# An LSTM layer on one core: gates regrouped into four equal banks, the cell state by a scan, x injected once per chunk

## What is computed

```
xW = einsum('ntd,dk->tnk', x, Wx) + b
a = xw_t + prev_h @ Wh                      # (4, 1024)
i = sigmoid(a[:, 0:H]);      f = sigmoid(a[:, H:2*H])
o = sigmoid(a[:, 2*H:3*H]);  g = tanh(a[:, 3*H:4*H])
next_c = f * prev_c + i * g
next_h = o * tanh(next_c)
return x + transpose(hs, (1, 0, 2))
```

## Time and profile before

| | |
|---|---|
| device time, median of 3 runs | 1141.09 us (1139.99 to 1141.9) |
| span of the profiled execution | 1138.7 us |
| instructions | 90172 |
| TensorE matmuls / weight loads busy | 915.0 us / 689.1 us |
| VectorE / ScalarE busy | 774.7 us / 395.4 us |
| DMA traffic | 8.72 MB, mean 8 GB/s |

### The profile page before, as it was taken

One profiled execution on the slowest core, in us unless ns is written; L12 is line 12 of the kernel. 1 busy time (PEld: TensorE's weight loads), 2 busy tenths in 40 slices (PEclk: granted clock), 3 DMA queues, 4 the chain that ended last, 5 costly groups with the idle time before them and its releaser, 6 DMA issues.

```text
span 1138.7 us, 90172 instructions
## 1 busy us (share of the span) xinstructions
PE 915.0 (80%) x38912; PEld 689.1 (61%) x38912; DVE 774.7 (68%) x4896; ACT 395.4 (35%) x2562; POOL 0.7 (0%) x6
## 2 busy tenths in 40 slices
PE   1888888888888888888888888888888888888886
PEld 1666666666666666666666666666666666666664
DVE  2676676676766766766766666767667666667665
ACT  0333333333333333333333333333333333333332
POOL 0000000000000000000000000000000000000000
PEclk9999999999999999999999999999999999999999
DMA  2000000000000000000000000000000000000000
GB/s 82 6 6 6 5 5 7 5 5 7 5 6 6 5 6 6 5 6 6 5 6 5 5 7 5 5 7 5 6 6 5 6 6 5 6 6 5 6 5 6
DMA packets 31868, 8.72 MB, mean 8 GB/s; under 512 B 31344, under 2 KB 31344, under 8 KB 31856
## 3 DMA queue, kind: packets, MB, share of 16 engines
q1 hardware_dynamic: 31248, 8.41, 3.1%
q10 hardware_dynamic: 608, 0.14, 0.1%
HBM read 6.43 MB, written 2.10 MB: 7 GB/s over the span
## 4 chain that ended last, share of the span: by engine, by line
DVE 42%; PE 39%; ACT 8%; issue 7%; DMA 2%; SPq 0%; DVEq 0%
PE gates L373 28%; DVE cell_bank L285 14%; DVE prods L290 9%; DVE cell_bank L303 8%; ACT acts L198 7%; PE gates_o L361 7%; DVE acts L297 5%; PE x_acc L343 5%; DVE h_units L308 3%; DVE x_part L226 2%; DMA wh_raw<-in_L_cond_Wh_dram 2%; DVE h_rows L261 1%; ACT cell_bank L206 1%; SPq L142 0%; SPq L136 0%
## 5 line engine op out<-in xcount | busy, mean ns | idle before, releaser
L373 PE MATMUL gates<-wh,h_units 128*4 128x96 f32 x16384 | 433.2, 247 | 49.9 <-DVE h_units L308 46.1
L373 PEld LDWEIGHTS gates<-wh,h_units 128*4 128x4 f32 x16384 | 311.1, 86 | 153.5 <-DVE h_units L308 149.2
L285 DVE STREAM_TRANSPOSE cell_bank<-gates 128x96 f32<-128x96 f32 x1024 | 243.0, 277 | 231.5 <-PE gates L373 230.6
L198 ACT ACTIVATE acts<-cell_bank 128x12 f32<-128x12 f32 x1024 | 177.5, 180 | 585.6 <-DVE cell_bank L285 576.9
L361 PE MATMUL gates_o<-x_part,ident 128*4 128x64 f32 x4096 | 151.3, 220 | 147.6 <-DVE cell_bank L303 147.6
L361 PE MATMUL gates<-x_part,ident 128*4 128x96 f32 x8192 | 264.0, 247 | 3.5 <-DVE x_part L226 3.5
L361 PEld LDWEIGHTS gates_o<-x_part,ident 128*4 128x4 f32 x4096 | 56.7, 84 | 269.1 <-DVE cell_bank L303 268.8
L373 PE MATMUL gates_o<-wh,h_units 128*4 128x64 f32 x8192 | 208.9, 219 | 0.0
L308 DVE SCALAR_TENSOR_TENSOR h_units<-tanh_o,cell_bank 128x4 f32<-128x4 f32 x1024 | 162.5, 159 | 44.4
L290 DVE SCALAR_TENSOR_TENSOR prods<-acts 128x8 f32<-128x8 f32 x1024 | 167.0, 163 | 36.6
L206 ACT ACTIVATE cell_bank<-acts 128x4 f32<-128x4 f32 x1024 | 178.8, 175 | 31.8
(11 more groups left out here) (22 smaller groups left out, 8.5 us busy)
## 6 DMA issues: line engine op xcount, KB each, us to landing
x_next<-in_x_dram SPq DMA_DIRECT2D x256, 8.0 KB
x_here<-in_x_dram SPq DMA_DIRECT2D x256, 8.0 KB
out_dram<-y_rows SPq DMA_DIRECT2D x256, 8.0 KB
wx_raw<-in_L_cond_Wx_dram SPq DMA_DIRECT2D x2, 512.0 KB
wh_raw<-in_L_cond_Wh_dram SPq DMA_DIRECT2D x2, 512.0 KB
bias_raw<-in_L_cond_b_dram ACTq DMA_DIRECT2D x4, 32.0 KB, 3.5
h_rows<-in_cond_dram ACTq DMA_DIRECT2D x4, 1.0 KB
```

The source lines that it names most:

```text
L198: nc.scalar.activation(acts[m][:, 0:len(IFG), :], turned[m].rearrange("p (g c) -> p g c", g=len(IFG))[:, :, 0:N], ACT.Tanh).then_inc(acts_ ...
L285: nc.vector.transpose(turned[m], gates[t % TURNS][m][:, 0:IC]).then_inc(gates_turned[m], 1)
L373: last = nc.tensor.matmul(bank[q * R:q * R + N, 0:columns.stop - columns.start], h_units[:, b, (t - 1) % STEPS, :], wh[:, b, q, columns], ...
```

## The change

The four gates go to four banks of 64 columns each: F of both halves (BF), G and I of half 0 (BA), G and I of half 1 (BB), O of both halves (BO). TensorE fills them in this order, and VectorE transposes each. The cell state of one half is made by one `tensor_tensor_scan` over K = 3 places for each of the 4 sequences: the running value is set to 1 (0 times the last, plus 1), then 1 times it plus tanh(i), then G times it plus the forget term. The forget term, (1 + tanh f) times half the old cell state, is one operation for both halves (`forget`). Half the cell state is made by ScalarE at the step's end (`half_d`).

The hidden state lies in `h_pad`, 4 columns of every 36, zeros between. A stationary operand is a window of 32 columns in which only the 4 of this step aren't zero, so a matmul adds nothing to the rows of the other steps. A bank holds all 8 steps of a chunk (32 rows per partition group), and the x part is injected once per chunk with an identity of 32 columns, at the last step, each bank behind its last transpose. `turn_back` goes ahead of the first transpose of step 0, and the pieces of the x product move one step later.

```diff
-    IFG = (I, F, G)
-    IC, OC = len(IFG) * R, M * R
-    GC = M * IC + OC
-    O_COLUMNS = slice(M * IC, GC)
-    TURNS = 2
+    W = M * R
+    BF, BA, BB, BO = range(4)
+    BANKS = (BF, BA, BB, BO)
+    GC = len(BANKS) * W
+    AB = (BA, BB)
     CHUNKS = T // STEPS
     DMA = 16
+    K = 3
+    WIN = R + N
     PIECES = [(b, slice(c * GC // 2, (c + 1) * GC // 2)) for b in range(M) for c in range(2)]
-    FIRST_PIECE_AT = 2
+    FIRST_PIECE_AT = 3
...
-        acts = [sb(f"acts{m}", [128, len(IFG) + 1, N]) for m in range(M)]
+        tanh_f = sb("tanh_f", [128, M, N])
         tanh_o = sb("tanh_o", [128, M, N])
-        prods = [sb(f"prods{m}", [128, 2, N]) for m in range(M)]
-        h_units = sb("h_units", [128, M, STEPS, N])
+        half_d = sb("half_d", [128, M, N])
+        scan_both = sb("scan_both", [128, M, 2 * K * N])
+        scan_in = [scan_both[:, m, :] for m in range(M)]
+        cell = sb("cell", [128, M, N, K])
+        h_pad = sb("h_pad", [128, M, (STEPS + 1) * WIN])
         h_rows = sb("h_rows", [128, QD])
         y_rows = sb("y_rows", [128, QD])
-        gates = [[ps(f"gates{b}{m}", [128, 512]) for m in range(M)] for b in range(TURNS)]
-        gates_o = ps("gates_o", [128, 512])
+        gates = [ps(f"gates{k}", [128, 512]) for k in BANKS]
         x_acc = ps("x_acc", [128, 512])
-        cell_bank = [ps(f"cell_bank{m}", [128, 512]) for m in range(M)]
-        turned = [cell_bank[m][:, 0:IC] for m in range(M)]
-        tanh_c = [cell_bank[m][:, IC:IC + N] for m in range(M)]
-        o_turned = cell_bank[0][:, GC // 2:GC // 2 + OC]
+        turned_bank = [ps(f"turned_bank{k}", [128, 512]) for k in range(3)]
+        turned = [turned_bank[k][:, 0:W] for k in (0, 1, 2)] + [turned_bank[0][:, W:2 * W]]
+        tanh_c = [turned_bank[AB[m]][:, W:W + N] for m in range(M)]
...
+        def columns_of(k):
+            return slice(k * W, (k + 1) * W)
+        def h_at(m, t):
+            at = (t % STEPS + 1) * WIN
+            return h_pad[:, m, at:at + N]
+        def h_stationary(m, t):
+            start = STEPS * WIN if t == 0 else t * R
+            return h_pad[:, m, start:start + R]
...
+            act.wait_ge(zeroed, 2)
+            def of_step(k, t):
+                return turned[k].rearrange("p (g c) -> p g c", g=M)[:, :, t * N:(t + 1) * N]
             with act.Fori(0, T, STEPS) as t0:
                 for t in range(STEPS):
+                    now = t0 + (t + 1)
+                    act.wait_ge(gates_turned[BF], now)
+                    nc.scalar.activation(tanh_f[:], of_step(BF, t), ACT.Tanh).then_inc(tanh_f_done, 1)
                     for m in range(M):
-                        act.wait_ge(gates_turned[m], t0 + (t + 1))
-                        nc.scalar.activation(acts[m][:, 0:len(IFG), :],
-                                             turned[m].rearrange("p (g c) -> p g c", g=len(IFG))[:, :, 0:N],
-                                             ACT.Tanh).then_inc(acts_done[m], 1)
-                    act.wait_ge(o_turn_done, t0 + (t + 1))
-                    nc.scalar.activation(tanh_o[:], o_turned.rearrange("p (m c) -> p m c", m=M)[:, :, 0:N],
-                                         ACT.Tanh)
+                        act.wait_ge(gates_turned[AB[m]], now)
+                        gap = K * N - 1
+                        at = K - 1
+                        ig = scan_in[m][:, at:at + 2 * gap].rearrange("p (g c) -> p g c", g=2)[:, :, 0:K * (N - 1) + 1:K]
+                        nc.scalar.activation(ig, of_step(AB[m], t), ACT.Tanh).then_inc(tanh_ig_done[m], 1)
+                    act.wait_ge(gates_turned[BO], now)
+                    nc.scalar.activation(tanh_o[:], of_step(BO, t), ACT.Tanh)
                     for m in range(M):
-                        act.wait_ge(c_done[m], t0 + (t + 1))
-                        nc.scalar.activation(tanh_c[m], acts[m][:, len(IFG), :], ACT.Tanh,
-                                             scale=0.5).then_inc(tanh_done[m], 1)
+                        act.wait_ge(cell_done[m], now)
+                        nc.scalar.activation(tanh_c[m], cell[:, m, :, K - 1], ACT.Tanh, scale=0.5).then_inc(tanh_done[m], 1)
+                    nc.scalar.activation(half_d[:], cell[:, :, :, K - 1], ACT.Copy, scale=0.5).then_inc(kept_done, 1)
...
+            nc.vector.memset(half_d[:], 0.0)
             for m in range(M):
-                nc.vector.memset(acts[m][:], 0.0)
-                for b in range(TURNS):
-                    nc.vector.memset(gates[b][m][:, 0:IC], 0.0)
-            nc.vector.memset(gates_o[:, 0:OC], 0.0).then_inc(zeroed, 1)
+                nc.vector.memset(scan_in[m][:, 0:K * N:K], 0.0)
+                nc.vector.memset(scan_in[m][:, 1:K * N:K], 1.0)
+                nc.vector.memset(scan_in[m][:, K * N:2 * K * N:K], 1.0)
+            nc.vector.memset(h_pad[:], 0.0).then_inc(zeroed, 1)
...
             def turn_back(chunk):
                 for m in range(M):
                     dve.wait_ge(h_done[m], chunk * STEPS + (STEPS + 1))
-                nc.vector.transpose(h_rows[:], h_units[:].rearrange("p m t n -> p (m t n)")).then_inc(h_turned_back, 1)
+                nc.vector.transpose(h_rows[:], h_pad[:, :, WIN:].rearrange("p m (t c) -> p m t c", c=WIN)[:, :, :, 0:N]
+                                    ).then_inc(h_turned_back, 1)
...
             def step(chunk, t, first, ahead):
                 now = chunk * STEPS + (t + 1)
+                if not first and t == 0:
+                    turn_back(chunk - 1)
                 if not first and t == 1:
                     residual(chunk - 1)
                 if ahead and t == 2:
                     dve.wait_ge(x_next_loaded, (chunk + 2) * (Q * DMA))
                     nc.vector.transpose(x_units[:], x_next[:]).then_inc(x_turned, 1)
                 if ahead and t == STEPS - 1:
-                    dve.wait_ge(injected, now)
                     make_x_part(chunk + 1)
...
+                def turn(k):
+                    dve.wait_ge(gates_done[k], now)
+                    nc.vector.transpose(turned[k], gates[k][:, 0:W]).then_inc(gates_turned[k], 1)
+                def forget():
+                    dve.wait_ge(tanh_f_done, now)
+                    nc.vector.scalar_tensor_tensor(out=scan_both[:, :, K * N + K - 1:2 * K * N:K], in0=tanh_f[:], scalar=1.0,
+                                                   in1=half_d[:], op0=ALU.add, op1=ALU.mult).then_inc(forgotten, 1)
+                def update(m):
+                    dve.wait_ge(tanh_ig_done[m], now)
+                    dve.wait_ge(forgotten, now)
+                    nc.vector.tensor_tensor_scan(cell[:, m, :, :].rearrange("p n k -> p (n k)"), scan_in[m][:, 0:K * N],
+                                                 scan_in[m][:, K * N:2 * K * N], 0.0, ALU.mult,
+                                                 ALU.add).then_inc(cell_done[m], 1)
                 def hidden(m):
                     dve.wait_ge(tanh_done[m], now)
-                    nc.vector.scalar_tensor_tensor(out=h_units[:, m, t, :], in0=tanh_o[:, m, :], scalar=1.0,
+                    nc.vector.scalar_tensor_tensor(out=h_at(m, t), in0=tanh_o[:, m, :], scalar=1.0,
                                                    in1=tanh_c[m], op0=ALU.add,
                                                    op1=ALU.mult).then_inc(h_done[m], 1)
-                turn(0)
-                if not first and t == 0:
-                    turn_back(chunk - 1)
-                turn(1)
-                product(0)
-                turn_o()
-                cell(0)
-                product(1)
-                cell(1)
+                turn(BF)
+                turn(BA)
+                turn(BB)
+                forget()
+                turn(BO)
+                update(0)
+                update(1)
                 hidden(0)
                 hidden(1)
...
+            def inject(k):
+                for q in range(Q):
+                    nc.tensor.matmul(gates[k][q * R:(q + 1) * R, 0:W], ident[:, q * R:(q + 1) * R],
+                                     x_part[:, columns_of(k)], start=True, stop=False,
+                                     tile_position=(0, q * R), skip_group_check=True)
...
             def step(chunk, t, ahead):
                 now = chunk * STEPS + (t + 1)
...
+                def recur(b, k):
                     for q in range(Q):
-                        last = nc.tensor.matmul(bank[q * R:q * R + N, 0:columns.stop - columns.start],
-                                                h_units[:, b, (t - 1) % STEPS, :], wh[:, b, q, columns],
-                                                start=False, stop=b == M - 1, tile_position=(0, q * R))
+                        last = nc.tensor.matmul(gates[k][q * R:(q + 1) * R, 0:W], h_stationary(b, t),
+                                                wh[:, b, q, columns_of(k)], start=False, stop=b == M - 1,
+                                                tile_position=(0, q * R), skip_group_check=True)
                     return last
```

(19 more changed lines are left out.)

60 lines of the change are left out of this document (14 added, 46 removed).

## The result

The changed kernel takes **1103.72 us**, median of 4 runs (1100.98 to 1106.8), against 1140.54 (1139.71 to 1141.9) before: ratio 0.968, 95% interval [0.9669, 0.9694]. It is faster by 36.8 us, inside the range, though 15 us above the forecast of 1089. That distance is not spread over the steps. The typical step got shorter than forecast (2.017 us against 2.05), and some steps are much longer. So the trace has to be read twice: a usual step, and a long one.

The account below looks back on a forecast made before the run. Bound by the latency of one step's chain, 2.16 us, times 512; terms sum to 2.05, so 1141.1 + 512 x (2.05 - 2.16) + 4 = 1089 us, range 1045 to 1140 (forecast's own range 1065 to 1115).

Parts of the forecast that it names:

- Latency bounds the kernel, not an engine's share: Whole kernel: TensorE busy 80% and VectorE 68%, neither full, so one step's length, 2.16 us, times 512 decides.
- Nine pitches of 0.0575, and 0.02 for the wide load: TensorE after the second hidden state: nine matmul groups take 0.52 us; the 32-column stationary's load adds 0.02 before the first.
- rival by loads: TensorE: 32-column loads not hidden beside matmuls stretch each pitch to 0.0815, step 2.27, 1201 us; chance 0.07.
- Transpose to tanh 0.31: From half 1's gate transpose on VectorE to its tanh on ScalarE: 0.31 us, taken between 0.29 and 0.33.
- Second wait 0.06: Scan on VectorE waits for two semaphores; the second was taken to add 0.06 us, bounds 0 and 0.08.
- Scan 0.20 to its tanh: From the scan's start on VectorE to the cell's tanh start: 0.20 us, bounds 0.19 and 0.30.
- Tanh to hidden state 0.21, and 0.16: Step's end: 0.21 us from the cell's tanh to the second hidden state, whose operation takes 0.16.
- VectorE's own way is shorter by 0.07: From half 1's transpose to the second scan: 1.41 through VectorE itself against 1.48 through ScalarE, so covered by 0.07.
- a sign of being wrong: Prediction called itself wrong if the second scan follows the first by VectorE's own pace rather than its tanh.
- turn_back and x_part, 4 us: VectorE, once a chunk, around F's transpose: 0.07 us a chunk, bounds 0 and 0.15, 4 us in all.
- one case, all steps at the lower clock or none: Clock rival: TensorE, idle some 1.1 us a step, stays at the lower clock; step 2.68, 1411 us, chance 0.03.
- injections go for nothing because they are off the chain: TensorE: injecting x's part every eighth step instead of every step brings no gain, lying beside the chain.

## Why the prediction was right, and where it failed

- **Latency bounds the kernel, not an engine's share.** Right. TensorE lost 213 us of busy time and the usual step lost 0.14 x 511 = 73 us, which is what was taken off the chain.
- **Nine pitches of 0.0575, and 0.02 for the wide load.** Right: the pitch is 0.056 with 4 columns and with 32, half 1's transpose stands 0.90 after the hidden state, and the four-column kernel gives back 0.02 to 0.03 a step. The rival by loads (pitch 0.0815, 1201 us) falls. The Trainium skill's rule behind it (TensorE: Matmul & The Clock Gate, "Part 3: Packing small matmuls"), that a load overlaps a running matmul only in another row group, is contradicted here: all four column tiles share the row group, and loads of 114 ns each go by at a pitch of 56 ns, so they stay hidden. The measurement decides.
- **Transpose to tanh 0.31.** 0.30.
- **Second wait 0.06.** Too much. Half 1's tanh to its scan is 0.23 where 0.21 + 0.06 was forecast, so it is 0.02, and taking this scan's second wait away changes the step by 0.003 at most.
- **Scan 0.20 to its tanh.** Too little by 0.03: 0.23. The scan takes 181 ns, where I would have had 163 + 4 x 1.1 = 167. The Trainium skill's half throughput (DVE: opcode table, instruction layouts, handler registers and perf-mode slots, "Datapath and trigger behaviour") gave an estimate of 12 ns more, 179, and the trace agrees with it, as far as one length of scan can: no run here has a longer or shorter one.
- **Tanh to hidden state 0.21, and 0.16.** 0.20 and 0.16. The measured sum is 0.90 + 0.30 + 0.23 + 0.23 + 0.20 + 0.16 = 2.02, against 2.05.
- **VectorE's own way is shorter by 0.07.** Here it is equal within 0.02: the second scan starts 0.10 behind the first, and also 0.05 behind the end of its tanh. I had named this as a sign of being wrong. VectorE's way runs through O's transpose, which the prediction counted there but called off the way: it waits for TensorE's last group of gates (563.52, 0.22 behind half 1's), and the first scan starts 0.21 behind it, not 0.17. Without its second wait the second scan still starts 0.10 behind the first, which fits two ways through the step that end together.
- **turn_back and x_part, 4 us.** Nothing: their steps take the usual 2.016. But step 4 of each chunk takes 2.13 instead of 2.017, 5 to 7 us in all, and nothing in my sum had it. In such a step O's transpose and the scans start late, by 0.12 together, with no wait that the profile names. Here O's transpose starts 0.12 behind forget and the first scan 0.25 behind it, where the usual step above has 0.05 and 0.21:

```profile
557.29 0.15 DVE L300 SCALAR_TENSOR_TENSOR scan_both<-tanh_f,half_d 128x8 f32<-128x8 f32 x1
557.41 0.27 DVE L295 STREAM_TRANSPOSE turned_bank<-gates 128x64 f32<-128x64 f32 x1
557.66 0.28 DVE L306 TENSOR_TENSOR_SCAN cell<-scan_both 128x12 f32<-128x12 f32 x2
```

In the two kernels with one wait less it lies in step 5 (2.10), and in the kernel with injections at every step, whose VectorE waits once more per chunk, in steps 5 and 6 (2.05 and 2.07). Step 4's work is the same in all of them, so it does not go with that; what happens there stays open.
- **The step that failed is the clock.** The prediction saw both facts: TensorE idle 1.1 us in each step, and a low clock at the start. It made of them one case, all steps at the lower clock or none, gave it 0.03 and put it at 1411. What happened lies between: 45 steps beyond the start, 28 us, the full ones 2.8 us long where it had worked out 2.68. With the usual step alone, and the 7 us of step 4 in every chunk, the kernel would take 1141.1 - 73 + 7 = 1075, and the filled kernels, at 1075 and 1079, show that time. The prediction's sentence that injections go for nothing because they are off the chain is true of the chain and left out what they do for the clock.

So the forecast came near by luck, for two reasons that offset each other: the usual step was cheaper than forecast by 17 us (0.033 x 512) and the chunk's 4 us did not come, while long steps and steps 4 to 6 were dearer by some 37 (30 and 7). The range, from the bounds of the other terms, held it; the mechanism behind the last 28 us had hardly any chance in it.

What stays open: why one chunk in three, and not all, has long steps with the same instructions in each; what the step-4 interval waits for; and what the move of the x pieces alone, or the products in another order, would have cost.

## What to carry to other kernels

Where TensorE runs in short bursts between waits, work beside the chain isn't free to remove: look at the granted clock in stretches before and after, and put independent matmuls into the bare stretches. Compare versions at equal clock by the interval from iteration to iteration, since the total mixes the chain with the clock. A chain that gets longer can cost more than its own length, when TensorE then idles more and its clock falls as well (395 us here, of which filling took 195 back). A shorter one does not give more back by itself: here the usual steps gave 73 us and the kernel 37.

## What the runs showed of the hardware that I had not expected

- In the stretch shown, the granted clock fell from 1.00 to 0.50 in the third step in a row in which TensorE had its 64 recurrent instructions alone, and a step then takes 0.78 us more: 2.80 against 2.02. Work that nobody reads took 25 us off the changed kernel, and some 195 off the one with products; taking off work added 84 us to the kernel before.
- A longer chain had more steps at the low clock: with 0.42 us more in it, long steps went from 49 to 282 of 511.
- TensorE can stand still for up to 5.2 us without a wait that the profile shows. The kernel in which it did moved 2.85 MB of instructions where the others moved 0.10 to 0.20; want of instructions is the likely cause, not a shown one.
- Two scans follow each other 0.10 apart on VectorE though each takes 0.18, while a product of 0.14 and the addition that needs it are 0.25 apart: what the dependency costs there is more than the operation.
